# Third-operand norms and a reordered prologue in an adaLN state-space and FFN layer

## The chip, the cores and the metric

The kernel runs on one core of one Trainium2 chip. The metric is the device time of one execution in microseconds. The kernel before was timed in three runs: 542.87 us in the median, 541.35 to 543.33.

## The reference, cut to what matters

The layer has four batches of 512 tokens and 256 channels, all in fp32.

```python
mod = (_silu(L0_c) @ L0_wmod).reshape(L0_c.shape[0], 6, 1, -1)
sa, ca, ga, sb, cb, gb = (mod[:, 0], ..., mod[:, 5])
h = _layernorm(x, axis=-1) * (1 + ca) + sa
x = x + ga * _L0_attn_ref(h, W_in, conv_w, conv_b, z_bias, D, W_out)
h = _layernorm(x, axis=-1) * (1 + cb) + sb
x = x + gb * _L0_ffn_ref(h, W1, W2, W3)
```

The first sub-layer projects h to x (256 columns), to B and C (32 heads of 64 states each), to z and to one number per head, A. x, B and C go through a causal convolution of four taps along the tokens. a = -softplus(A), its running sums give decays exp(segsum(a)), and y is the sum over earlier tokens of (C . B) times the decay times x. Then y times silu(z) goes through W_out. The second sub-layer is a gated FFN with a Walsh-Hadamard transform in the hidden dimension of 1024. ga and gb are kept at least 0.25 away from zero.

## The kernel before, in words

Each engine has an order of work written out by hand, in its own block, and the engines meet through semaphores that count finished instructions. The program has three stages. The prologue (to about 56 us) normalises the input, computes h for all four batches, the x projection, its convolution, the projection A with its running sums and decays. The main loop goes over 16 half-groups of heads (NG groups, B batches each) in which B and C are projected, convolved and used. The last stage is the output projection, the second norm and the FFN.

In fp32 the products on TensorE are made of three passes. Every operand is split into a high part (rounded to the fast fp32r type) and a low part (the rest), and `split_mm` (L369) adds high weights x high h, high weights x low h, and low weights x high h. The parts of h are `ht_hi` and `ht_lo`; those of the x weights `wx_hi` and `wx_lo`.

The prologue, batch by batch, is a pipeline over the engines:

- VectorE: `statistics1(b)` (bn_stats, bn_aggr, variance + eps, L1053 to L1059), then `normalise1(b)` (L1066), four instructions of 128 x 256, that subtract the mean and multiply by `rstd`. `modulation(0)` copies shift and scale out of PSUM (L1096, L1097). Afterwards the taps of the x convolution (L1089), the softplus sum (`sp_a`, L1133), the scan of the running sums (L1137), and so on to the taps of the first B and C (L1177).
- GpSimd: `inverse_root(b)` (L1404) makes `rstd`, the weights of x are split at L1415 and L1417, `h_low(b, kt)` (L1409) makes the low part of h, `split_tile` (L1397, L1399) splits the weights of B and C, L1434 and L1436 those of z.
- TensorE: `norm_transposes(b)` (L396, eight transposes), filler products of zeros in `warm(n)` (L468), `x_project(b, xt)` (L410, six matmuls), `a_project(b0)` (L426, eight matmuls for two batches), `x_transposes`, `p_transposes` (L451, transposes of the running sums).
- ScalarE: `h_full(b, kt)` (L764) makes h in fp32 with scale and shift out of PSUM, `h_high(b, kt)` (L770) its high part, `x_tap(b, xt)` (L777) the last tap with bias. Then the absolute value (L810), exponential (L812) and logarithm (L815) of the softplus.

The waits that matter here: `h_full` waits for the transposes of its batch and for shift and scale (`mod_ev`); for batches 2 and 3 its slot of h32 has to be free too. `h_low` waits for `h_high`. `x_project(b, xt)` waits for both low parts of its batch, and from batch 2 on for the taps that read its PSUM bank two batches earlier. `a_project(2)` waits for h32 of batches 2 and 3. ScalarE's L810 waits for all the a products, and `x_tap(2, 0)` stands behind it in ScalarE's order.

The order on TensorE from the first transposes on is: transposes 0 and 1, ten fillers, `a_project(0)`, transposes 2, x of batch 0, transposes 3, x of batch 1, `a_project(2)`, `x_project(2, 0)`, the modulation for the second norm, and then transposes of x mixed with the rest of the x products and the transposes of the running sums. The second norm uses the same `normalise` helper, as `normalise2(b)`, once per batch (L1066 too), and its transposes are at L677.

Of the kernel before, what the change touches and what calls it, by code (L numbers as in the profile page):

```python
# [15 lines left out]
ALU = mybir.AluOpType  # L16
ACT = mybir.ActivationFunctionType

P = 128
B, L, D = 4, 512, 256  # L20
# [3 lines left out]
KT = D // P  # L24
# [4 lines left out]
GT = 4  # L29
# [21 lines left out]
def adaln_ssm_ffn_kernel(nc, u, w_bc, w_x, w_a, w_z, conv, d_rows, z_bias, w_out, w13, w2, c_t, wmod,  # L51
                         consts, out, e_d, gates_d):
    with ExitStack() as ctx:
        def sb(name, shape, dt, where=ctx):
            return where.enter_context(nc.sbuf_tensor(name, shape, dt))

        def sem(name):
            return ctx.enter_context(nc.semaphore(name))

        ps = ctx.enter_context(nc.psum_tensor("ps", [P, 8, BANK], F32))  # L60


        ht_hi = sb("ht_hi", [P, KT, B * L], F32R)
        ht_lo = sb("ht_lo", [P, KT, B * L], F32R)
# [12 lines left out]
        meanvar = sb("meanvar", [P, 2, CH, 2], F32)  # L77
        vareps = sb("vareps", [P, 2, CH], F32)
        rstd = sb("rstd", [P, 2, CH], F32)
# [14 lines left out]
        wx_hi = sb("wx_hi", [P, 2, KT, P], F32R, reg_a)  # L94
        wx_lo = sb("wx_lo", [P, 2, KT, P], F32R, reg_a)
# [45 lines left out]
        xt = sb("xt", [P, KT, L], F32)  # L141
# [32 lines left out]
        s = {n: sem(n) for n in names}  # L174
# [191 lines left out]
        def _(pe):  # L366
            mm = nc.tensor.matmul
# [21 lines left out]
            def norm_transposes(b):  # L389

                pe.wait_ge(s["xn_done"], CH * (b + 1))
                if b >= 2:
                    pe.wait_ge(s["h32_done"], KT * (2 * b - 3))
                for c in range(CH):
                    for kt in range(KT):
                        i = nc.tensor.transpose(ps[:, (4 if b == 1 else 2) + kt, c * P:(c + 1) * P],  # L396
                                                xn[:, b % 2, c, kt * P:(kt + 1) * P], ident)
                i.then_inc(s["lnT_mm"], 1)
# [11 lines left out]
            def x_project(b, xt):  # L410

                pe.wait_ge(s["hlo_done"], KT * (b + 1))
                if b >= 2:
                    pe.wait_ge(s[f"xtaps{xt}"], 3 * (b - 1))
                for kt in range(KT):
                    i = split_mm(ps[:, GT * (b % 2) + xt, :], wx_hi[:, xt, kt, :], wx_lo[:, xt, kt, :],
                                 ht_hi[:, kt, b * L:(b + 1) * L], ht_lo[:, kt, b * L:(b + 1) * L],
                                 kt == 0, kt == KT - 1)
                i.then_inc(s["xp_mm"], 1)

            def a_project(b0):

                pe.wait_ge(s["h32_done"], KT * (b0 + 2))
                for kt in range(KT):
                    for b in (b0, b0 + 1):
                        i = mm(ps[b * NH:(b + 1) * NH, 6, :], wa_sb[:, kt, :], h32[:, b % 2, kt, :],  # L426
                               start=(kt == 0), stop=(kt == KT - 1), skip_group_check=True)
                        if kt == KT - 1:
                            i.then_inc(s["a_mm"], 1)
# [35 lines left out]
            def warm(n):  # L465

                for k in range(n):
                    mm(ps[:, 1, :], zeros[:, 0:P], zeros[:], start=True, stop=True)  # L468
# [19 lines left out]
            pe.wait_ge(s["ld_ident"], 16)  # L488
            norm_transposes(0)
            norm_transposes(1)  # L490
            warm(10)
            pe.wait_ge(s["ld_wa"], 16)
            a_project(0)
            norm_transposes(2)
            pe.wait_ge(s["mod_ev"], 2)
            pe.wait_ge(s["wx_split"], 2)
            x_project(0, 0)
            x_project(0, 1)
            norm_transposes(3)
            x_project(1, 0)  # L500
            x_project(1, 1)
            a_project(2)
            x_project(2, 0)
            pe.wait_ge(s["ld_wmod2"], 16)
            modulation((3, 4), 7)
            x_transposes(0, 0)
# [244 lines left out]
        def _(act):  # L751
# [5 lines left out]
            def h_full(b, kt):  # L757

                n = KT * b + kt
                act.wait_ge(s["lnT_mm"], b + 1)  # L760
                if b >= 2:
                    act.wait_ge(s["hlo_done"], n - 3)
                    act.wait_ge(s["a_mm"], 2)
                af(h32[:, b % 2, kt, :], ps[:, (4 if b == 1 else 2) + kt, :], ACT.Identity, bias=shift[:, 0, kt, b:b + 1],  # L764
                   scale=scale1[:, 0, kt, b:b + 1]).then_inc(s["h32_done"], 1)

            def h_high(b, kt):

                act.wait_ge(s["h32_done"], KT * b + kt + 1)
                nc.scalar.copy(ht_hi[:, kt, b * L:(b + 1) * L], h32[:, b % 2, kt, :]).then_inc(s["hhi_done"], 1)  # L770

            def x_tap(b, xt):

                n = 2 * b + xt
                act.wait_ge(s["xp_mm"], n + 1)
                w = conv_sb[:, NG * GT + xt, :]
                af(acc[:, n // GT, n % GT, :], ps[:, GT * (b % 2) + xt, :], ACT.Identity, bias=w[:, TAPS:TAPS + 1],  # L777
                   scale=w[:, TAPS - 1:TAPS]).then_inc(s["xtap"], 1)
# [7 lines left out]

            act.wait_ge(s["mod_ev"], 2)
            h_full(0, 0)
            h_full(0, 1)
            h_full(1, 0)  # L790
            h_high(0, 0)
            h_full(1, 1)
            h_high(0, 1)
            h_high(1, 0)
            h_high(1, 1)
            h_full(2, 0)
            h_high(2, 0)
            h_full(2, 1)
            act.wait_ge(s["ld_conv"], 16)
            x_tap(0, 0)  # L800
            h_high(2, 1)
            x_tap(0, 1)
            h_full(3, 0)
            h_full(3, 1)
            x_tap(1, 0)
            x_tap(1, 1)
            h_high(3, 0)
            h_high(3, 1)
            act.wait_ge(s["a_mm"], B)
# [225 lines left out]
        def _(dve):  # L1035
            ts = nc.vector.tensor_scalar
            tt = nc.vector.tensor_tensor
            stt = nc.vector.scalar_tensor_tensor
# [22 lines left out]
            def normalise(src, dst, n, names):  # L1061

                st, ag, ep, rs, done = names
                dve.wait_ge(s[rs], n + 1)
                for c in range(CH):
                    ts(dst[:, c, :], src[:, c, :], meanvar[:, n % 2, c, 0:1], rstd[:, n % 2, c:c + 1], ALU.subtract,  # L1066
                       ALU.mult).then_inc(s[done], 1)

            norm1_names = ("bnst", "bnag", "eps1", "rs", "xn_done")
            norm2_names = ("bn2", "ag2", "eps2", "rs2", "xn2_done")  # L1070
# [5 lines left out]
            def normalise1(b):  # L1076
                if b >= 2:
                    dve.wait_ge(s["lnT_mm"], b - 1)
                normalise(u_sb[:, b * CH:(b + 1) * CH, :], xn[:, b % 2], b, norm1_names)
# [12 lines left out]
            def modulation(n):  # L1092

                dve.wait_ge(s["mod_mm"], 4 * (n + 1))
                mod = ps[:, 7 * n, 0:2 * KT * B].rearrange("p (k m b) -> p k m b", k=2, m=KT)
                nc.vector.tensor_copy(shift[:, n], mod[:, 0]).then_inc(s["mod_ev"], 1)  # L1096
                ts(scale1[:, n], mod[:, 1], 1.0, None, ALU.add).then_inc(s["mod_ev"], 1)  # L1097
# [10 lines left out]
            statistics1(0)  # L1108
            statistics1(1)
            normalise1(0)  # L1110
            normalise1(1)
            modulation(0)
            statistics1(2)
            statistics1(3)
            normalise1(2)
# [247 lines left out]
        def _(pool):  # L1363
# [28 lines left out]
            def split_tile(g, t):  # L1392

                if not (isinstance(g, int) and g == 0) and t < 2:
                    await_unit("w_high_act", g * 2 + PLACE[t] - 1)
                else:
                    gp.tensor_copy(wg_hi[:, t], wg_raw[:, t]).then_inc(s["w_high"], 1)  # L1397
                    await_unit("w_high", g * 2 + PLACE[t] + 1)
                gp.tensor_tensor(wg_lo[:, t], wg_raw[:, t], wg_hi[:, t].bitcast(F32), ALU.subtract).then_inc(s["w_split"], 1)  # L1399

            def inverse_root(n, eps_name, name):

                await_unit(eps_name, n + 1)
                gp.tensor_tensor(rstd[:, n % 2], vareps[:, n % 2], minus_half[:], ALU.pow).then_inc(s[name], 1)  # L1404

            def h_low(b, kt):

                pool.wait_ge(s["hhi_done"], KT * b + kt + 1)
                gp.tensor_tensor(ht_lo[:, kt, b * L:(b + 1) * L], h32[:, b % 2, kt, :],  # L1409
                                 ht_hi[:, kt, b * L:(b + 1) * L].bitcast(F32), ALU.subtract).then_inc(s["hlo_done"], 1)  # L1410
# [4 lines left out]
            gp.tensor_copy(wx_hi[:], wx_raw[:]).then_inc(s["wx_split"], 1)  # L1415
            pool.wait_ge(s["wx_split"], 1)
            gp.tensor_tensor(wx_lo[:], wx_raw[:], wx_hi[:].bitcast(F32), ALU.subtract).then_inc(s["wx_split"], 1)  # L1417
            inverse_root(2, "eps1", "rs")
            inverse_root(3, "eps1", "rs")
            h_low(0, 0)  # L1420
            h_low(0, 1)
            h_low(1, 0)
            h_low(1, 1)
            h_low(2, 0)
            pool.wait_ge(s["ld_wg"], 16)
            split_tile(0, 1)
            h_low(2, 1)
            split_tile(0, 0)
            h_low(3, 0)
# [229 lines left out]
```

## Time and profile before

| what | value |
|---|---|
| median of three runs | 542.87 us (541.35 to 543.33) |
| profiled execution | 541.1 us, span 538.9 us |
| mean granted clock of TensorE | 0.996 |
| TensorE busy | 528.2 us (98%) |
| VectorE busy | 455.3 us (84%) |
| ScalarE busy | 372.5 us (69%) |
| GpSimd busy | 241.0 us (45%) |
| one tap of a convolution on VectorE (L1177), mean of 384 | 0.741 us |

Busy time is the sum in which an engine had an instruction under way. A busy TensorE isn't one at its peak, since its matmuls overlap. The span is the time from the first to the last instruction of the profiled execution, and the rest of its time lies around it.

### The profile page before, as it was taken

To read this page: it belongs to the slowest core of one execution; us is meant where nothing else is said; L and a number is where in the kernel's file an instruction comes from. 1 tells how busy PE (TensorE), PEld (TensorE's weight loads), DVE (VectorE), ACT (ScalarE), POOL (GpSimd) and SP (SyncE) were. 2 spreads that over 40 slices of the span, in tenths; PEclk is the share of its full clock that TensorE was granted. 3 is DMA by queue.
4 is the path that set the end of the run, shared out by engine and by line. 5 is a ranking of instruction groups with operands and counts; after the bars stand their busy time and mean duration, and the time that the engine had idled before them with its cause. 6 is when DMAs were issued, how large, how long until landed. Compare 5 with 4: busy or idle time off the path is not lost.

```text
span 538.9 us, 19393 instructions
## 1 busy us (share of the span) xinstructions
PE 528.2 (98%) x7188; PEld 427.2 (79%) x7188; DVE 455.3 (84%) x746; ACT 372.5 (69%) x988; POOL 241.0 (45%) x465
## 2 busy tenths in 40 slices
PE   6999999999999999999999999999999999999997
PEld 3667777878878878877877877876889889889886
DVE  6999999999999999999999999999756657657342
ACT  1778998898898898898898898887534234234240
POOL 5863374776776775776775574484000000000000
PEclk9999999999999999999999999999999999999999
DMA  7737443432423425423423424566531322100101
GB/s 261 286 110 224 122 112 98 141 83 95 138 79 95 138 80 176 134 83 95 134 84 95 132 85 138 166 196 191 160 80 38 79 78 79 40 1 1 40 0 40
DMA packets 50289, 59.40 MB, mean 110 GB/s; under 512 B 8004, under 2 KB 44740, under 8 KB 49864
## 3 DMA queue, kind: packets, MB, share of 16 engines
q1 hardware_dynamic: 50248, 58.88, 36.0%
q8 instruction: 22, 0.36, 0.3%
q14 instruction: 19, 0.16, 0.1%
HBM read 48.75 MB, written 9.05 MB: 107 GB/s over the span
## 4 chain that ended last, share of the span: by engine, by line
PE 92%; DVE 4%; ACT 2%; issue 1%; DMA 1%; POOL 0%; SPq 0%; ACTq 0%; DVEq 0%; POOLq 0%
PE ps L371 20%; PE ps L372 20%; PE ps L373 20%; PE ps L550 10%; PE ps L531 6%; PE ps L600 4%; PE ps L586 3%; PE ps L569 3%; PE ps L667 3%; DVE acc L1177 2%; PE ps L396 1%; PE ps L613 1%; DMA u_sb<-in_u 1%; PE ps L426 1%; PE ps L677 1%
## 5 line engine op out<-in xcount | busy, mean ns | idle before, releaser
L1177 DVE SCALAR_TENSOR_TENSOR acc<-ps,cw_dve,acc 128x511 f32<-128x511 f32 (+2 forms) x384 | 257.8, 741 | 3.5 <-ACT acc L834 3.0
L868 ACT ACTIVATE decay<-sums,p_slot 128x128 f32<-128x128 f32 (+1 forms) x512 | 147.0, 370 | 2.2 <-ACT p_slot L943 1.0
L1478 POOL TENSOR_TENSOR sums<-sums,far_above 128x256 f32<-128x256 f32 x128 | 96.0, 753 | 117.4 <-DMA sums<-packed_sums 111.0
L834 ACT ACTIVATE acc<-ps,cw_act 128x512 f32<-128x512 f32 x128 | 93.0, 776 | 28.5 <-PE ps L600 26.4
L371 PE MATMUL ps<-ht_hi,wg_hi 128*128 128x512 f32 x256 | 107.1, 419 | 0.1
L372 PE MATMUL ps<-ht_lo,wg_hi 128*128 128x512 f32 x256 | 101.2, 395 | 0.0
L373 PE MATMUL ps<-ht_hi,wg_lo 128*128 128x512 f32 x256 | 101.2, 395 | 0.0
L1003 ACT ACTIVATE silu_sb<-ps 128x512 f32<-128x512 f32 x32 | 19.2, 599 | 77.8 <-PE ps L373 77.8
L1165 DVE TENSOR_TENSOR mix<-ps,decay 128x768 f32<-128x768 f32 x64 | 60.9, 952 | 6.1 <-PE ps L550 5.2
L1404 POOL TENSOR_TENSOR rstd<-vareps,minus_half 128x4 f32<-128x4 f32 x8 | 8.4, 1048 | 119.4 <-DVE vareps L1059 117.1
L550 PE MATMUL ps<-acc 64*64 64x128 f32 (+1 forms) x2048 | 57.6, 249 | 0.8
L373 PEld LDWEIGHTS ps<-ht_hi,wg_lo 128*128 128x128 f32 x256 | 48.1, 188 | 11.6
L1316 DVE TENSOR_TENSOR hid<-ps,silu_sb 128x512 f32<-128x512 f32 x32 | 22.1, 692 | 40.4 <-ACT silu_sb L1003 40.3
L371 PEld LDWEIGHTS ps<-ht_hi,wg_hi 128*128 128x128 f32 x256 | 48.2, 188 | 9.6 <-issue 0.4
L372 PEld LDWEIGHTS ps<-ht_lo,wg_hi 128*128 128x128 f32 x256 | 48.5, 189 | 8.5
L550 PEld LDWEIGHTS ps<-acc 64*64 64x64 f32 x2048 | 48.8, 133 | 7.0 <-issue 2.5
L371 PE MATMUL ps<-h_hi,w_hi 128*128 128x512 f32 x128 | 50.5, 394 | 0.0
L373 PE MATMUL ps<-h_hi,w_lo 128*128 128x512 f32 x128 | 49.9, 390 | 0.0
L372 PE MATMUL ps<-h_lo,w_hi 128*128 128x512 f32 x128 | 49.9, 390 | 0.0
L371 PE MATMUL ps<-w_hi,hid_hi 128*128 128x256 f32 x128 | 36.9, 289 | 0.2 <-DVE stage L1332 0.2
L372 PE MATMUL ps<-w_lo,hid_hi 128*128 128x256 f32 x128 | 36.2, 283 | 0.0
L373 PE MATMUL ps<-w_hi,hid_lo 128*128 128x256 f32 x128 | 36.2, 283 | 0.0
(143 smaller groups left out, 889.8 us busy)
## 6 DMA issues: line engine op xcount, KB each, us to landing
sums<-packed_sums SPq DMA_DIRECT2D x256, 96.0 KB, 2.7
wg_raw<-in_w_bc SPq DMA_DIRECT2D x8, 512.0 KB, 4.2
y_parts<-yt_sb SPq DMA_DIRECT2D x64, 64.0 KB, 2.0
stage<-y_parts SPq DMA_DIRECT2D x32, 128.0 KB, 2.8
u_sb<-in_u SPq DMA_DIRECT2D x4, 512.0 KB, 4.4
stage<-in_w SPq DMA_DIRECT2D x1, 2048.0 KB, 11.6
x_channels<-acc SPq DMA_DIRECT2D x8, 256.0 KB, 2.6
ee<-running_sums SPq DMA_DIRECT2D x8, 256.0 KB, 3.7
```

What stands on the lines that cost most here:

```text
L371: mm(o, w_hi, x_hi, start=first, stop=False)
L372: mm(o, w_hi, x_lo, start=False, stop=False)
L373: return mm(o, w_lo, x_hi, start=False, stop=last)
L531: i = nc.tensor.transpose(ps[:, 6, c * P:(c + 1) * P], acc[:, b % 2, p, c * P:(c + 1) * P], ident)
L550: i = mm(ps[NS * at:NS * (at + 1), 2 + a, o:o + P - NS * h], acc[own, b % 2, p, c * P + NS * h:c * P + NS * (h + 1)], acc[own, b % 2, 2 + ...
L600: i = mm(ps[QD * quarter:QD * (quarter + 1), 7, k * P + NS * h:(k + 1) * P], xs[:, b % 2, w:w + QD], mix[:, j, k * PW + NS * (1 - h):k * P ...
L834: af(acc[:, b % 2, t, :], ps[:, PROJ_BANK[t], :], ACT.Identity, bias=cw_act[:, t, 1:2], scale=cw_act[:, t, 0:1]).then_inc(s[f"tap_a{t}"], 1)
L868: i = af(decay[:, j, own], sums[:, j, own], ACT.Exp, scale=-1.0, bias=p_slot[:, b * CH + n, j:j + 1])
L1165: tt(mix[:, 2 * p:2 * p + 2, 0:PL], ps[:, 2:4, 0:PL], decay[:, 2 * p:2 * p + 2, 0:PL], ALU.mult).then_inc(s["mixed"], 1)
L1177: stt(a[:, d:], ps[:, PROJ_BANK[t], 0:L - d], cw_dve[:, t, TAPS - 1 - d:TAPS - d], a[:, d:], ALU.mult, ALU.add).then_inc(s[f"taps{t}"], 1)
L1316: tt(hid[:, m % 2, :], ps[:, 2 + m % 2, :], silu_sb[:, m % 2, :], ALU.mult).then_inc(s["hid_done"], 1)
L1478: gp.tensor_tensor(v, v, far, ALU.add).then_inc(s["masked"], 1)
```

## The change

It has five parts. (1) `normalise` uses scalar_tensor_tensor, with `rstd` broadcast along 256 columns as a third operand, instead of tensor_scalar with two per-partition scalars; the mean stays such a scalar. It serves both norms. (2) VectorE copies the modulation between the norms of batch 0 and batch 1. (3) On TensorE two new functions make the x product in two passes, first all that uses the high part of h, and later what uses the low part; batches 0 and 1 go by them. Six of ten fillers go, `a_project(0)` stands between the two passes of batch 0, transposes 2 behind them, and `x_project(2, 0)` ahead of `a_project(2)`. (4) ScalarE's order follows: the high part right behind the full one for batch 0, and the taps ahead of the next batch's h. (5) On GpSimd the low parts of batch 0 go in front of the inverse roots of batches 2 and 3, and the first weight split ahead of the low part (2, 0).

```diff
+            def x_project_high(b):
+                pe.wait_ge(s["hhi_done"], KT * (b + 1))
+                for xt in range(2):
+                    for kt in range(KT):
+                        o, x = ps[:, GT * (b % 2) + xt, :], ht_hi[:, kt, b * L:(b + 1) * L]
+                        mm(o, wx_hi[:, xt, kt, :], x, start=(kt == 0), stop=False, skip_group_check=True)
+                        mm(o, wx_lo[:, xt, kt, :], x, start=False, stop=False, skip_group_check=True)
+            def x_project_low(b):
+                pe.wait_ge(s["hlo_done"], KT * (b + 1))
+                for xt in range(2):
+                    for kt in range(KT):
+                        i = mm(ps[:, GT * (b % 2) + xt, :], wx_hi[:, xt, kt, :], ht_lo[:, kt, b * L:(b + 1) * L],
+                               start=False, stop=(kt == KT - 1), skip_group_check=True)
+                    i.then_inc(s["xp_mm"], 1)
...
             norm_transposes(1)
-            warm(10)
+            warm(4)
+            pe.wait_ge(s["mod_ev"], 2)
+            pe.wait_ge(s["wx_split"], 2)
+            x_project_high(0)
             pe.wait_ge(s["ld_wa"], 16)
             a_project(0)
+            x_project_low(0)
             norm_transposes(2)
-            pe.wait_ge(s["mod_ev"], 2)
-            pe.wait_ge(s["wx_split"], 2)
-            x_project(0, 0)
-            x_project(0, 1)
+            x_project_high(1)
+            x_project_low(1)
             norm_transposes(3)
-            x_project(1, 0)
-            x_project(1, 1)
+            x_project(2, 0)
             a_project(2)
-            x_project(2, 0)
...
             h_full(0, 0)
+            h_high(0, 0)
             h_full(0, 1)
+            h_high(0, 1)
             h_full(1, 0)
-            h_high(0, 0)
             h_full(1, 1)
-            h_high(0, 1)
             h_high(1, 0)
             h_high(1, 1)
-            h_full(2, 0)
-            h_high(2, 0)
-            h_full(2, 1)
             act.wait_ge(s["ld_conv"], 16)
             x_tap(0, 0)
+            x_tap(0, 1)
+            h_full(2, 0)
+            h_full(2, 1)
+            h_high(2, 0)
             h_high(2, 1)
-            x_tap(0, 1)
+            x_tap(1, 0)
+            x_tap(1, 1)
             h_full(3, 0)
             h_full(3, 1)
-            x_tap(1, 0)
-            x_tap(1, 1)
...
-                    ts(dst[:, c, :], src[:, c, :], meanvar[:, n % 2, c, 0:1], rstd[:, n % 2, c:c + 1], ALU.subtract,
-                       ALU.mult).then_inc(s[done], 1)
+                    stt(dst[:, c, :], src[:, c, :], meanvar[:, n % 2, c, 0:1], rstd[:, n % 2, c:c + 1].to_broadcast([P, D]),
+                        ALU.subtract, ALU.mult).then_inc(s[done], 1)
...
             normalise1(0)
+            modulation(0)
             normalise1(1)
-            modulation(0)
...
+            h_low(0, 0)
             inverse_root(2, "eps1", "rs")
+            h_low(0, 1)
             inverse_root(3, "eps1", "rs")
-            h_low(0, 0)
-            h_low(0, 1)
             h_low(1, 0)
             h_low(1, 1)
-            h_low(2, 0)
             pool.wait_ge(s["ld_wg"], 16)
             split_tile(0, 1)
+            h_low(2, 0)
             h_low(2, 1)
```

## Rows read from the trace of the kernel before

**Rows 1.** The page, the chain that ended last, by engine.

```profile
PE 92%; DVE 4%; ACT 2%; issue 1%; DMA 1%; POOL 0%; SPq 0%; ACTq 0%; DVEq 0%; POOLq 0%
```

**Rows 2.** Stages: length; PE, PEld, DVE, ACT, POOL busy (instructions); clock, DMA share, GB/s.

```profile
12.84:14.60 1.76, 1.76 (x8) 1.70 (x9) 1.73 (x10) 1.45 (x2) 0.00 (x0) 0.50 1.02 389
14.60:17.60 3.00, 3.00 (x13) 1.10 (x11) 2.96 (x13) 2.75 (x5) 1.68 (x2) 0.76 0.66 250
...
67.00:357.00 290.00, 289.37 (x5329) 232.72 (x5333) 281.21 (x405) 258.14 (x766) 190.27 (x384) 1.00 0.38 114
```

**Rows 3.** Timeline of TensorE: start, length, line, count, idle before.

```profile
12.84 1.97 PE L396 MATMUL ps<-cst,xn 128*128 128x128 f32 x8 [1.45 <-DVE xn L1066]
14.60 3.04 PE L468 MATMUL ps<-sums 128*128 128x512 bf16 x10
17.58 1.91 PE L426 MATMUL ps<-h,wa_sb 128*32 128x512 f32 x8
19.42 1.09 PE L396 MATMUL ps<-cst,xn 128*128 128x128 f32 x8
20.62 0.47 PE L371 MATMUL ps<-ht_hi,wx_hi 128*128 128x512 f32 x1
...
23.51 1.03 PE L396 MATMUL ps<-cst,xn 128*128 128x128 f32 x8
...
27.29 1.91 PE L426 MATMUL ps<-h,wa_sb 128*32 128x512 f32 x8
...
35.73 1.09 PE L451 MATMUL ps<-cst,sums_t 128*64 128x128 f32 x16 [0.19 <-DVE sums_t L1137]
```

**Rows 4.** Timeline of VectorE, the norms, the taps and the scan.

```profile
8.80 3.99 DVE L1066 TENSOR_SCALAR xn<-u_sb,meanvar,rstd 128x256 f32<-128x256 f32 x8
...
10.72 1.42 DVE L1066 TENSOR_SCALAR xn<-u_sb,meanvar,rstd 128x256 f32<-128x256 f32 x1
...
18.20 5.01 DVE L1066 TENSOR_SCALAR xn<-u_sb,meanvar,rstd 128x256 f32<-128x256 f32 x4 [0.15 <-POOL rstd L1404]
...
34.37 1.22 DVE L1137 TENSOR_TENSOR_SCAN sums_t<-reset,sp_a 128x512 f32<-128x512 f32 x1
...
43.76 7.31 DVE L1177 SCALAR_TENSOR_TENSOR acc<-ps,cw_dve,acc 128x511 f32<-128x511 f32 x11 [0.23 <-ACT acc L834]
```

**Rows 5.** Line L1066 alone (ns min/median/max), and ScalarE's timeline.

```profile
L1066 DVE TENSOR_SCALAR xn<-x_tok,meanvar,rstd x16: 406/408/411, 375.4 to 492.6; 128x256 f32<-128x256 f32 x16
...
15.52 0.61 ACT L770 CAST ht_hi<-h 128x512 fp32r<-128x512 f32 x1
16.03 0.78 ACT L764 ACTIVATE h<-ps,shift,scale 128x512 f32<-128x512 f32 x1
...
29.27 0.60 ACT L810 ACTIVATE a_work<-ps 128x512 f32<-128x512 f32 x1
...
30.84 0.78 ACT L777 ACTIVATE acc<-ps,conv_sb 128x512 f32<-128x512 f32 x1 [0.30 <-PE ps L373]
```

**Rows 6.** A third-operand form on VectorE, GpSimd beside it, and line L1478.

```profile
354.64 0.74 DVE L1198 SCALAR_TENSOR_TENSOR stage<-xt,d_ch,stage 128x512 f32<-128x512 f32 x1
...
360.10 1.00 DVE L1198 SCALAR_TENSOR_TENSOR stage<-xt,d_ch,stage 128x512 f32<-128x512 f32 x1
...
360.50 1.20 POOL L1478 TENSOR_TENSOR sums<-sums,far_above 128x256 f32<-128x256 f32 x1
...
L1478 POOL TENSOR_TENSOR sums<-sums,far_above x128: 724/738/1286, 42.3 to 371.3; 128x256 f32<-128x256 f32 x128
```

**Rows 7.** Timeline of GpSimd: weight splits and low parts.

```profile
10.73 1.26 POOL L1417 TENSOR_TENSOR wx_lo<-wx_raw,wx_hi 128x512 fp32r<-128x512 f32 x1
...
17.92 6.44 POOL L1409 TENSOR_TENSOR ht_lo<-h,ht_hi 128x512 fp32r<-128x512 f32 x5
...
34.45 2.20 POOL L1436 TENSOR_TENSOR wz_lo<-wz_raw,wz_hi 128x512 fp32r<-128x512 f32 x1
```

**Rows 8.** Waits from 360 us on: total, times, longest.

```profile
PEld ps L677 <- DVE xn L1066: 0.2, 1, 0.2
```

## The prediction

> **What bounds the kernel now.** I read the chain of waits first: 92% of it is TensorE's [rows 1]. The stage table then shows TensorE busy for 289.37 of 290.00 us in the main loop, with VectorE at 281.21 [rows 2]. All the edits but the second norm's lie ahead of that loop, so they can only move the moment at which it begins, and the time is as long as that moment is late. The timeline of TensorE comes next. From 12.84 us on it has next to no idle time, but not all of it is needed: ten filler products run from 14.60 to 17.6 us (3.04 us, 0.30 each), because the first x product waits for the low part of h [rows 3]. The granted clock is low there: 0.50 from 12.84 to 14.60 us and 0.76 over 14.60 to 17.60, that is 1.2 GHz first and 2.4 GHz later. TensorE sat idle for 1.45 us ahead of it, from 11.39 to 12.84 us [rows 2, 3]. VectorE is the other one without slack: it is delayed in the fourth norm (four instructions in 5.01 us, where the 16 of the later norm take 0.41 us each) and then runs taps almost without a break, until the scan at 34.37 us releases TensorE's transposes at 35.73 us and eleven taps from 43.76 us on lie in the chain [rows 3, 4, 5]. So TensorE's order, VectorE's order and the softplus chain (a products, ScalarE, scan, transposes) are nearly co-critical, and an edit has to move all three forward to gain.
>
> **The norm with a third operand.** The nearest row of that form is the 128x512 one at 354.64 us: 0.74 us [rows 6]. Half of its columns, at 0.96 a ns, are 0.27 us, so 128x256 takes about 0.48. Eleven taps of 0.741 us (table of the profile) fill 7.31 us, so instructions start 0.66 apart and overlap by 0.08 [rows 4]: 0.40 from start to start, against 0.41 less 0.08, 0.33, now. That is +0.07 us each. Bounds: 0 (it costs what tensor_scalar costs) and 0.33 (the 512-column form whole).
>
> What could pay for it is VectorE no longer standing behind GpSimd. The rows show that standing: one norm instruction takes 1.42 us beside the split of wx (1.26 us), and the fourth norm's four take 5.01 us beside low parts of 1.29 us [rows 4, 7]. But instructions that read two SBUF tensors stand in the same way: the 128x512 form took 1.00 us at 360.10 beside GpSimd work, and the GpSimd mask at 360.50 took 1.20 against a median of 0.738 us; the scan at 34.37 ran beside a GpSimd subtraction of 2.20 us whose twin takes 1.26 [rows 4, 6, 7]. The new form reads two SBUF tensors (u_sb and the broadcast rstd). I take it that it is held too, and, being longer, holds GpSimd by about 0.1 us more.
>
> The Trainium skill ("SBUF — State Buffer", section "SBUF: two separate sides") says that the port pair of VectorE and GpSimd is an exclusive lock, taken by a VectorE instruction in a two-port mode or with two SBUF inputs against a GpSimd instruction that reads SBUF. By that rule the third operand takes the norm out of one clause and puts it into the other; the rows above agree.
>
> In time: the first norm ends at 8.80 + 3 x 0.40 + 0.48 = 10.48 us, against 10.18 (8.80 + 3 x 0.32 + 0.41). The modulation copies (two, of 8 columns each) go next, so they are done at 10.6 instead of 12.9 us. Of the second norm's four, the first starts at 10.6 and pushes the split of wx from about 11.99 to 12.3 us, the second ends at 12.6, the others at 13.0 and 13.4. The second transposes start at 13.5 instead of 12.84 us: +0.65.
>
> **The x products with high h first, and the low parts in front.** ScalarE may start at 11.7 us, when the first transposes are done (11.39 + 0.3). A full h is 0.78 us, a high part 0.61, and now each high part waits for its full one: both high parts of batch 0 stand at about 11.7 + 2 x (0.78 + 0.61) = 14.5 us [rows 5]. TensorE isn't there yet: transposes 1.76 us at the low clock to 15.26, four fillers at 0.43 (twice the 0.213 that 512 columns take at 2.4 GHz) to 17.0. Then eight high products at 0.24 (twelve take 2.89 [rows 3]) to 18.9, the a products 1.84 to 20.7, four low products 0.95 to 21.7. The low part of h is ready long before: GpSimd had nothing to do from 12.84 to 14.60 us [rows 2], where the low part (0, 0) goes (1.29 us), and (0, 1) follows the third inverse root and ends near 17.6 us. So its wait is gone. No DMA is moved and SyncE's order is the same. The fourth inverse root comes later by what is left of that low part, about 0.7 us. The fourth norm, which ended at 18.20 + 5.01 = 23.2 us, I expect to end near 23.6; the fourth transposes need it at 25.6, and x_project(2, 0) needs the fifth tap behind it, at 23.6 + 5 x 0.66 = 26.9. Both are covered, by 2 and by 0.5 us; past that each us costs a us.
>
> What is late next are the third transposes. They stood behind the a products alone and ended at 20.5 us; now they stand behind both x parts as well and end at 21.7 + 1.03 = 22.7 us [rows 3]. So h of batch 2 is 2.2 us later: full parts 22.75 to 24.2 (overlapping by 0.1), high parts to 25.3, low parts 24.8 to 27.4 (2 x 1.29). The first weight split has moved ahead of them and ends before 24.8. TensorE in that time does x of batch 1 (12 x 0.24) and the fourth transposes, to about 26.5, then idles 0.9 us, where it had no wait at all. x_project(2, 0) runs 27.4 to 28.85 us.
>
> **The a products moved behind it.** They used to run from 27.29 to 27.29 + 1.84 = 29.13 us; now from 28.85 to 30.7 [rows 3], +1.55. ScalarE's absolute value and exponential wait for them and x_tap(2, 0) behind those: it began 1.57 us after the absolute value, 0.30 of that idle, so 30.75 + 1.27 = 32.0 instead of 30.84 us, then the table load and the logarithm [rows 5]. So the idle 0.30 takes in a part of the +1.55, and 0.1 is rounding. The three taps, sp_a and the scan follow, so the transposes of the sums start at 35.73 + 1.15 = 36.9 us. From there the order on every engine is as before, and neither has idle time to take it in. Bounds: 0 (x of batch 2 not late) and 1.6 (nothing taken in).
>
> **The norms of the second half.** +0.07 x 4 per batch. TensorE waits once for this norm, 0.2 us, at batch 0, and not at the others, which are hidden by the down projection [rows 8]. So up to 0.3 there; I take 0.2.
>
> **Sum.** +1.15 + 0.2 = +1.35. The profiled execution took 541.1 us (span 538.9), 1.8 below the median of 542.87; 541.1 + 1.35 = 542.45, on the median's footing 544.2. A measurement can tell about 0.5% here, 2.7 us, so I call this no change, on the slow side.
>
> **Rivals.**
> *A wash.* The third operand is not held by GpSimd. The second norm ends at 10.6 + 3 x 0.40 + 0.48 = 12.3, its transposes start at 12.4, x of batch 0 is done by 12.4 + 1.76 + 1.7 + 1.9 + 1.84 + 0.95 = 20.5, 1.2 us ahead of the forecast, so the a products of batch 2 end at 29.5 instead of 29.13 us; VectorE leaves the fourth norm near 19.5. With 0.2 for the later norm the end is +0.2 to +0.4: 543.1 us. For it: nothing but the different form; against it the three cases in the rows. 0.20.
>
> *The fillers come off whole.* Six fillers at 0.30 are 1.8 us of TensorE's gapless stretch. If the second transposes are not later and the batch-2 chain finds cover, all behind moves by -1.8, with the later norm -1.6: 541.3 us. For it speaks that TensorE has no idle time between 12.84 and 35.5; against it that VectorE and the a products must come forward too. 0.15.
>
> *The slow side: the clock stays low.* The idle time ahead of the second transposes grows from 1.45 to 1.8 us and there are six fewer fillers, so that the products of x run at 1.2 GHz: the eight high ones cost 1.9 us more, which is paid in full since TensorE paces the third transposes. It decides from the point where the granted clock is still at 0.5 after 17.0 us. 544.2 + 1.9 = 546.1 us. For it: the clock was low behind such a gap [rows 2]; against it: it came back within the fillers' stretch, and the work is as dense. 0.12.
>
> **How the numbers follow.** Forecast 0.50, wash 0.20, fillers 0.15, low clock 0.12, others 0.03. The range is 541.0 to 546.1: the fillers' case to the low clock's, with half a us of run noise below. Slower by over 0.5% (above 545.6): half of the low-clock case, a tenth of the forecast: 0.11. Faster by over 0.5% (below 540.2): a third of the fillers' case and a little noise, 0.06. Within: 0.83.
>
> **What would show it.** Norm instructions near 0.48 us alone and 1.3 to 1.5 us beside GpSimd's low parts; the second transposes at 13.5; third transposes ending at 22.7; a gap on TensorE ahead of x_project(2, 0), released by a low part; the scan at 35.5. The forecast is wrong if norms beside low parts take 0.5 us, if the scan starts at or before 34.4, or if the time falls below 542.

## The result and the profile after

The changed kernel took 543.12 us in the median of 22 runs (542.0 to 544.14), the kernel before 541.71 us in 22 (540.62 to 543.65). The ratio is 1.0023, 95% interval [1.0014, 1.0032]: 1.2 us slower, 0.8 to 1.7. The forecast was +1.35. The three runs of the prediction had put the kernel before at 542.87 us, 1.2 above its median of 22, so only differences are compared below, and not times. The profiled execution took 542.87 us, its span is 540.7.

TensorE's timeline after the change (start, length, line, count, idle before and its releaser); x_project_high is at L427 and L428, x_project_low at L435, the a products at L444, the transposes of the sums at L469:

```profile
10.75 1.06 PE L396 MATMUL ps<-cst,xn 128*128 128x128 f32 x8 [1.84 <-DVE xn L1084]
13.61 1.97 PE L396 MATMUL ps<-cst,xn 128*128 128x128 f32 x8 [1.79 <-DVE xn L1084]
15.37 1.60 PE L486 MATMUL ps<-sums 128*128 128x512 bf16 x4
16.62 0.58 PE L427 MATMUL ps<-ht_hi,wx_hi 128*128 128x512 f32 x1
...
18.76 1.91 PE L444 MATMUL ps<-h,wa_sb 128*32 128x512 f32 x8
20.60 1.18 PE L435 MATMUL ps<-ht_lo,wx_hi 128*128 128x512 f32 x4
21.62 1.03 PE L396 MATMUL ps<-cst,xn 128*128 128x128 f32 x8
...
27.44 0.48 PE L371 MATMUL ps<-ht_hi,wx_hi 128*128 128x512 f32 x1 [1.10 <-POOL ht_lo L1427]
...
37.04 1.09 PE L469 MATMUL ps<-cst,sums_t 128*64 128x128 f32 x16 [1.73 <-DVE sums_t L1155]
```

Against [rows 3]: the idle time ahead of the second transposes is 1.79 instead of 1.45 us, there is a new gap of 1.10 us ahead of x_project(2, 0), released by a low part, and one of 1.73 us ahead of the transposes of the sums, where 0.19 stood. Those start 1.31 us later than before.

VectorE, and its norm line (ns min/median/max):

```profile
8.94 1.67 DVE L1084 SCALAR_TENSOR_TENSOR xn<-u_sb,meanvar,rstd 128x256 f32<-128x256 f32 x4
...
10.67 2.88 DVE L1084 SCALAR_TENSOR_TENSOR xn<-u_sb,meanvar,rstd 128x256 f32<-128x256 f32 x4
...
17.78 5.97 DVE L1084 SCALAR_TENSOR_TENSOR xn<-u_sb,meanvar,rstd 128x256 f32<-128x256 f32 x8
...
32.96 2.06 DVE L1107 SCALAR_TENSOR_TENSOR acc<-ps,conv_sb,acc 128x511 f32<-128x511 f32 x3 [1.73 <-ACT acc L795]
...
L1084 DVE SCALAR_TENSOR_TENSOR xn<-u_sb,meanvar,rstd x16: 473/479/1511, 8.9 to 22.8; 128x256 f32<-128x256 f32 x16
```

GpSimd's low parts (two in 2.92 us beside the norm) and its line of all eight:

```profile
19.10 2.92 POOL L1427 TENSOR_TENSOR ht_lo<-h,ht_hi 128x512 fp32r<-128x512 f32 x2
...
L1427 POOL TENSOR_TENSOR ht_lo<-h,ht_hi x8: 1272/1290/1479, 13.4 to 32.3; 128x512 fp32r<-128x512 f32 x8
```

The new form takes 0.479 us alone and up to 1.51 beside GpSimd, where tensor_scalar had 0.41 and 1.42 [rows 4, 5], and the low part beside it takes 1.48 instead of 1.29. I call an instruction held when it is longer than alone because it has to wait for the other engine. The granted clock, by stretch:

```profile
13.30:15.10 1.80, 1.49 (x7) 1.50 (x8) 1.80 (x9) 1.34 (x3) 1.28 (x1) 0.50 1.05 415
15.10:17.00 1.90, 1.90 (x8) 1.05 (x7) 1.86 (x10) 1.39 (x3) 1.42 (x2) 0.62 0.72 196
```

An estimate from these rows and from [rows 2]: 0.50 over 1.80 us and 0.62 over 1.90 are 1.80 + 1.44 = 3.2 us at 1.2 GHz, and in the kernel before 1.76 + 1.44 = 3.2 as well (0.50 over 1.76 us, 0.76 over 3.00). In these two executions the low stretch has the same length, and only comes about 0.5 us later.

The main loop is as it was (289.45 of 290 us busy). Not all of the 1.8 us between the spans is the prologue's. The first norm starts 0.14 us later, at 8.94, before anything changed is met, and at the loop's end 0.67 us of waiting for a tap stand where there was none:

```profile
361.24 0.47 PE L371 MATMUL ps<-ht_hi,wz_hi 128*128 128x512 f32 x1 [0.67 <-DVE acc L1195]
```

That wait was 0.15 us or absent in the profiles of the experiments, so I take it to belong to that execution. I therefore compare prologues by the distance from the first norm instruction to the transposes of the sums.

### The profile page after: what moved, and what is told of

Read it like the earlier page. It is cut to its first block, busy times and chain, and to the rows that moved or that the text cites. A ratio compares the mean times of both kernels' runs of the same rounds, so it can differ in the third digit from the quotient of the medians.

```text
span 540.7 us, 19381 instructions
## 1 busy us (share of the span) xinstructions
PE 526.2 (97%) x7182; PEld 426.8 (79%) x7182; DVE 457.0 (85%) x746; ACT 372.2 (69%) x988; POOL 240.5 (44%) x465
## 4 chain that ended last, share of the span: by engine, by line
PE 90%; DVE 5%; ACT 2%; issue 1%; DMA 1%; POOL 0%; SPq 0%; DVEq 0%; ACTq 0%
PE ps L371 20%; PE ps L372 19%; PE ps L373 19%; PE ps L568 9%; PE ps L549 5%; PE ps L618 4%; PE ps L587 3%; PE ps L604 3%; PE ps L685 3%; DVE acc L1195 2%; DVE xn L1084 1%; DMA u_sb<-in_u 1%; PE ps L631 1%; PE ps L695 1%; PE ps L444 1%
## 5 line engine op out<-in xcount | busy, mean ns | idle before, releaser
L1496 POOL TENSOR_TENSOR sums<-sums,far_above 128x256 f32<-128x256 f32 x128 | 94.4, 741 | 120.5 <-DMA sums<-packed_sums 112.1
L371 PE MATMUL ps<-w_hi,hid_hi 128*128 128x256 f32 x128 | 36.9, 289 | 0.2 <-DVE stage L1350 0.2
```

Of the source, the lines that this page charges most:

```text
L371: mm(o, w_hi, x_hi, start=first, stop=False)
L1496: gp.tensor_tensor(v, v, far, ALU.add).then_inc(s["masked"], 1)
```

## The experiments

"Distance" is that distance in the one profiled execution, against 26.93 us in the kernel before (35.73 - 8.80), and "clock" the mean granted clock of that execution (0.996 in the kernel before): a distance also holds what the clock cost there. "Total" is the ratio's distance from 1 times 541.7 us.

| kernel | ratio to the kernel before, 95% | total, us | distance, against before | clock |
|---|---|---|---|---|
| changed | 1.0023 [1.0014, 1.0032] | +1.2 | 28.10, +1.2 | 0.997 |
| e1 third operand alone | 1.0027 [1.0016, 1.0039] | +1.5 | 28.12, +1.2 | 0.994 |
| e2 changed, scalar norms | 0.9990 [0.9976, 1.0004] | -0.5 | 26.19, -0.7 | 1.000 |
| e3 changed, a products first | 1.0027 [1.0007, 1.0046] | +1.5 | 28.0, +1.1 | 0.996 |
| e4 changed, operand in PSUM | 0.9987 [0.9978, 0.9997] | -0.7 | 26.70, -0.2 | 0.997 |
| e5 e2, no overlap in norm 1 | 0.9976 [0.9965, 0.9986] | -1.3 | 25.87, -1.1 | 1.000 |
| e6 e5, reordered for batch 2 | 1.0003 [0.9990, 1.0016] | +0.2 | 28.45, +1.5 | 0.996 |
| e7 changed, ten fillers | 1.0036 [1.0023, 1.0049] | +2.0 | 29.64, +2.7 | 0.997 |
| e8 changed, tap before softplus | 1.0015 [1.0005, 1.0025] | +0.8 | 28.69, +1.8 | 0.993 |
| e9 e5, taps and h of batch 2 interleaved | 0.9986 [0.9976, 0.9996] | -0.8 | 25.90, -1.0 | 1.000 |
| e10 changed, no overlap in norm 1 | 1.0020 [1.0007, 1.0032] | +1.1 | 28.24, +1.3 | 1.000 |
| e11 e9, scan without overlap | 0.9976 [0.9965, 0.9987] | -1.3 | 25.91, -1.0 | 0.995 |
| e12 before, no overlap in norm 1 | 0.9982 [0.9968, 0.9996] | -1.0 | 26.13, -0.8 | 1.000 |

**e1, the third operand alone.**

```diff
 (kernel before)
-                    ts(dst[:, c, :], src[:, c, :], meanvar[..., 0:1], rstd[..., c:c + 1], ALU.subtract, ALU.mult)
+                    stt(dst[:, c, :], src[:, c, :], meanvar[..., 0:1], rstd[..., c:c + 1].to_broadcast([P, D]),
+                        ALU.subtract, ALU.mult)
```

> The kernel before with the one edit of the third operand in both norms. Theory (the new form is held by GpSimd as the old one was, and is longer): the second transposes start about 0.6 us later than 12.84, the fourth norm takes 5.9 us instead of 5.01 and each low part beside it 1.46 instead of 1.29 us, and the total is +0.8 to +1.2 us against the kernel before. Rival (all the loss is the order of the a products): 0.0 to +0.2 us. Second rival (the new form is free of GpSimd): the fourth norm takes 1.7 us, and the total is -0.3 to +0.2.

Measured: +1.5 us. The second transposes start at 13.35, the third and fourth norm together take

```profile
17.12 7.36 DVE L1066 SCALAR_TENSOR_TENSOR xn<-u_sb,meanvar,rstd 128x256 f32<-128x256 f32 x8
```

where they took 1.38 and 5.01 us. The two had started at 16.67 us and ended at 23.21 there, gap included. So this one edit makes as much as the whole change, and a little more than I had expected of it (0.8 to 1.2).

**e2, scalar norms in the changed order.** The edit of e1 undone in the changed kernel.

> The changed kernel with tensor_scalar back in both norms, all else changed. Theory: the second transposes start 0.6 us earlier than in the changed kernel (13.0), and the whole chain down to the scan moves with them: -0.5 to -0.8 us against the changed kernel, still +0.4 to +0.7 above the kernel before. Rival (order of the a products alone): no difference from the changed kernel.

Measured: -0.5 us against the kernel before (interval from -1.3 to +0.2), so about 1.8 us below the changed kernel, more than twice what I had expected. The transposes are 0.6 us earlier, as said; what I had not counted is in these rows:

```profile
13.07 1.09 PE L396 MATMUL ps<-cst,xn 128*128 128x128 f32 x8 [1.46 <-DVE xn L1084]
...
18.77 3.17 DVE L1084 TENSOR_SCALAR xn<-u_sb,meanvar,rstd 128x256 f32<-128x256 f32 x4 [0.16 <-POOL rstd L1422]
...
25.62 0.47 PE L371 MATMUL ps<-ht_hi,wx_hi 128*128 128x512 f32 x1 [1.21 <-DVE acc L1107]
```

The fourth norm ends near 21.9 instead of 23.7 us and frees VectorE for the taps, which are now what x_project(2, 0) waits for; and the transposes ran at 2.4 GHz in this execution (1.09 instead of 1.97 us). The mean granted clock was 1.000 in 6 of 11 runs (540.3 to 541.1 us) and 0.994 or 0.996 in the others (541.7 to 542.6). Of the changed kernel's 22 runs none had 1.000, and ten had 0.993 (543.0 to 543.7 us).

**e3, the a products first.**

```diff
 (changed kernel)
-            x_project(2, 0)
             a_project(2)
+            x_project(2, 0)
```

> The changed kernel with a_project(2) back in front of x_project(2, 0). a_project(2) then waits for the full h of batch 3, at 27.9 us, and ends at 29.8 instead of 31.0; x_project(2, 0) ends at 31.3, x_tap(2, 0) starts near 31.4 instead of 32.2, and the scan moves by the same. Theory (the softplus chain sets the end): -0.6 to -0.9 us against the changed kernel. Rival (TensorE's sum of work sets it): 0 to +0.4, since TensorE now idles 1.5 us instead of 1.1 ahead of these products.

Measured: +1.5 us against the kernel before, no gain on the changed one; the interval is wide (seven runs). The a products run earlier, but into a wait for h of batch 3, and VectorE's scan is longer:

```profile
27.94 1.91 PE L444 MATMUL ps<-h,wa_sb 128*32 128x512 f32 x8 [1.63 <-ACT h L782]
...
36.67 1.09 PE L469 MATMUL ps<-cst,sums_t 128*64 128x128 f32 x16 [0.73 <-DVE sums_t L1155]
```

```profile
35.01 1.51 DVE L1155 TENSOR_TENSOR_SCAN sums_t<-reset,sp_a 128x512 f32<-128x512 f32 x1
```

The scan starts 0.4 us nearer to the first norm than in the changed kernel (26.35 against 26.74), but it takes 1.51 us instead of 1.21, since it stood behind GpSimd's subtraction for the z weights. The expectation of -0.6 to -0.9 fell.

**e4, the third operand in PSUM.** The first norm multiplies by zeros left in PSUM by the first fillers; the multiplication by rstd is left out in it.

```diff
 (changed kernel)
-            warm(20)
+            warm(20, 7).then_inc(s["filled"], 1)
...
+                    factor = ps[:, 7, 0:D] if done == "xn_done" else rstd[:, n % 2, c:c + 1].to_broadcast([P, D])
```

> The changed kernel, but the third operand of the first norm is read from PSUM (zeros of the first twenty fillers, now in bank 7) in place of rstd, so the multiplication by rstd is left out there; the instruction has the same form and length and one SBUF input. Theory (two SBUF inputs are what holds it): 0.48 us each also beside GpSimd work, the second norm ends near 12.3, the fourth takes 1.7 us, low parts take 1.29 us, the second transposes start at 12.4 instead of 13.6: -1.0 to -1.3 us against the changed kernel. Rival (any long VectorE instruction that reads SBUF is held): as the changed kernel.

Measured: -0.7 us against the kernel before, about 1.9 below the changed one, more than the 1.0 to 1.3 expected. The same form, with one SBUF tensor instead of two:

```profile
L1088 DVE SCALAR_TENSOR_TENSOR xn<-u_sb,meanvar,ps x16: 470/472/479, 9.0 to 20.3; 128x256 f32<-128x256 f32 x16
...
17.54 3.22 DVE L1088 SCALAR_TENSOR_TENSOR xn<-u_sb,meanvar,ps 128x256 f32<-128x256 f32 x8
```

```profile
18.79 2.53 POOL L1431 TENSOR_TENSOR ht_lo<-h,ht_hi 128x512 fp32r<-128x512 f32 x2
```

No instruction of sixteen is held (479 ns at most, 1511 in the changed kernel), and the low parts beside them are back at 1.27 us. That is the mechanism shown: it is the second SBUF input that meets GpSimd, not the length or the form. The edit also takes the broadcast away, but that isn't what is held: the scan (L1155) reads two whole SBUF tensors, and takes 1.51 us in e3 and 1.66 in e8 beside a GpSimd subtraction, where it takes 1.21 alone. Since everything behind this norm works on other numbers in e4, I lean on the length of its instructions and less on its total. The Trainium skill ("SBUF — State Buffer", section "SBUF: two separate sides") states the lock for just this case, two SBUF inputs against a GpSimd instruction that reads SBUF. This trace agrees, with 1511 ns at most for two SBUF inputs and 479 for one. What the change took out by leaving tensor_scalar's form, which was held too (1.42 us), it put back with the broadcast operand.

**e5, no overlap in the second norm.**

```diff
 (e2)
+            act.wait_ge(s["ld_wx"], 16)
+            nc.scalar.copy(wx_hi[:], wx_raw[:]).then_inc(s["wx_split"], 1)
...
-            gp.tensor_copy(wx_hi[:], wx_raw[:]).then_inc(s["wx_split"], 1)
+            pool.wait_ge(s["xn_done"], 2 * CH)
```

> tensor_scalar norms in the changed order; ScalarE (idle there) makes the high part of the x weights, and GpSimd starts their low part only when the second norm is done. Theory (what VectorE loses to GpSimd in the second norm sets the start of the second transposes): they start at 12.1 to 12.3 us instead of 13.07 in the kernel with scalar norms, the gap on TensorE ahead of them shrinks from 1.45 to 0.6 us, and the granted clock stays nearer 1.0; behind that h of batch 0 (ready at 14.5) sets the high x products, so -0.3 to -0.8 us against that kernel, -0.8 to -1.3 against the kernel before. Rival (later steps set all): no difference from the kernel with scalar norms.

Measured: -1.3 us against the kernel before, as expected. The gap ahead of the second transposes is 0.30 us, and the clock was 1.000 in 8 of 12 runs:

```profile
11.69 1.09 PE L396 MATMUL ps<-cst,xn 128*128 128x128 f32 x8 [0.30 <-DVE xn L1086]
...
34.67 1.09 PE L469 MATMUL ps<-cst,sums_t 128*64 128x128 f32 x16 [1.72 <-DVE sums_t L1157]
```

**e6, reordered for batch 2.** e5 with the third transposes ahead of x_project_low(0), h of batch 2 ahead of the taps of batch 0 on ScalarE, the low parts of batch 2 ahead of the first weight split, x_tap(2, 0) ahead of the absolute value.

> As the last one, with the third transposes ahead of x_project_low(0), ScalarE's h of batch 2 ahead of the taps of batch 0, the low parts of batch 2 ahead of the first weight split, and x_tap(2, 0) ahead of the absolute value. Theory (the changed kernel loses on the way third transposes, h of batch 2, x_project(2, 0), a products, scan): no gap ahead of x_project(2, 0), transposes of the sums at 33.5 to 34.3 instead of 35.73 us in the kernel before, total -1.5 to -2.3 us against the kernel before. Rival (VectorE's taps set it): they start at 21 to 22 us and the transposes of the sums come at 35 or later, total -0.8 or less.

Measured: +0.2 us against the kernel before, so 1.5 us worse than e5. The low part was ready at 24.5 us, and x_project(2, 0) waited for its PSUM bank instead:

```profile
26.92 0.47 PE L371 MATMUL ps<-ht_hi,wx_hi 128*128 128x512 f32 x1 [2.51 <-DVE acc L1109]
```

```profile
23.14 9.54 DVE L1109 SCALAR_TENSOR_TENSOR acc<-ps,conv_sb,acc 128x511 f32<-128x511 f32 x14 [1.25 <-ACT acc L795]
```

The taps of batch 0 had been put behind h on ScalarE; the rival named that. Behind that wait the granted clock fell once more, from about 27.7 to 31 us (0.50 over 28.00 to 31.00), and four of the a products took 1.59 us there, where they take 1.03 in the changed kernel:

```profile
29.96 1.59 PE L444 MATMUL ps<-h,wa_sb 128*32 128x512 f32 x4
```

How much of the 1.5 us is the wait and how much the clock, no run tells.

**e7, ten fillers.** `warm(10)` for `warm(4)` in the changed kernel.

> The changed kernel with ten fillers instead of four. Theory (TensorE paces the way to the third transposes): the high x products start 1.3 to 2.0 us later and the whole is +1.3 to +1.8 us against the changed kernel. Rival (the fillers keep the clock up and pay for themselves): the mean granted clock is higher than in the changed kernel (0.993 in half of its runs) and the total within 0.5 us of it.

Measured, by five runs: +2.0 us against the kernel before, 0.7 above the changed one, with clocks of 0.997 in four of them. The distance grows by 1.5 us in the one profile. The loss lies between the two expectations. The fillers delay the x products, and the higher mean clock did not pay for them: the four runs at 0.997 took 544.0 to 544.5 us and the fifth, at 0.993, 543.3.

**e8, x_tap(2, 0) ahead of the softplus.**

```diff
 (changed kernel)
+            x_tap(2, 0)
             act.wait_ge(s["a_mm"], B)
...
-            x_tap(2, 0)
             act.wait_ge(s["aexp_done"], 1)
```

> The changed kernel with one move: ScalarE's x_tap(2, 0) ahead of the absolute value, which waits for the a products. Theory (VectorE's idle 1.7 us ahead of its three taps and sp_a behind them are on the path): the idle time goes, sp_a starts when the logarithm ends, 34.2 instead of 34.94 us, and the total is -0.5 to -0.8 us against the changed kernel; a collision of the scan with the split of the z weights, as it cost 0.3 us with the a products first, may take back 0.3. Rival (the a products alone set it): 0.

Measured: +0.8 us against the kernel before, 0.4 below the changed kernel, with intervals that overlap. The expected 0.5 to 0.8 isn't shown. The distance is long because the profiled execution had the clock at 1.2 GHz until about 18.4 us (mean 0.993), which delayed the x products; it says nothing of the edit. VectorE's idle time moved behind the taps, and the collision I had named was larger, 0.45 instead of 0.3 us:

```profile
35.07 0.69 DVE L1151 SCALAR_TENSOR_TENSOR sp_a<-ps,a_work 128x512 f32<-128x512 f32 x1 [1.91 <-ACT a_work L833]
...
35.82 1.66 DVE L1155 TENSOR_TENSOR_SCAN sums_t<-reset,sp_a 128x512 f32<-128x512 f32 x1
```

**e9, taps and h interleaved.** e5 with the third transposes ahead of x_project_low(0), ScalarE's full h (2, 0), (2, 1), high (2, 0), tap (0, 0), high (2, 1), tap (0, 1), VectorE's taps of (0, 0) first, and the low parts of batch 2 ahead of the first weight split.

> The kernel with scalar norms and no overlap in the second norm, with the third transposes ahead of x_project_low(0), ScalarE's order full h (2, 0), (2, 1), high (2, 0), tap (0, 0), high (2, 1), tap (0, 1), VectorE's three taps of (0, 0) first, and the low parts of batch 2 ahead of the first weight split. Theory (x_project(2, 0) is held by two waits, the low part and the PSUM bank that the taps of (0, 0) still read, and both must move): it starts at 24.1 to 24.4 instead of 25.07 us and the transposes of the sums come 0.5 to 0.9 us earlier than in that kernel; total -1.6 to -2.1 us against the kernel before. Rival (VectorE, which now idles until 22.1 us, or the waits behind 50 us take it back): -1.3 or less.

Measured: -0.8 us against the kernel before; the interval overlaps that of e5. x_project(2, 0) starts at 24.41, but then the scan takes 1.67 us beside GpSimd. The gain stays below 1.3 us as the rival said, and the scan's hold is what the trace shows for it.

**e10, third operand without overlap in the second norm.** The edit of e5 in the changed kernel.

> The changed kernel, third operand kept, but ScalarE makes the high part of the x weights and GpSimd starts their low part behind the second norm. Theory (the third operand costs by its hold in the second norm and so by the start of the second transposes; its hold in the fourth norm is covered): the second norm takes 1.67 us, the second transposes start at 12.6 instead of 13.6 us, -0.8 to -1.2 us against the changed kernel, near the kernel before. Rival (the fourth norm's hold, 6 us, is what costs): no gain against the changed kernel.

Measured: +1.1 us, no gain that shows on the changed kernel; my expectation fell, and the rival, the fourth norm's hold, held. The second transposes do start at 12.00, but

```profile
27.19 0.47 PE L371 MATMUL ps<-ht_hi,wx_hi 128*128 128x512 f32 x1 [2.40 <-DVE acc L1109]
```

```profile
17.51 5.99 DVE L1086 SCALAR_TENSOR_TENSOR xn<-u_sb,meanvar,rstd 128x256 f32<-128x256 f32 x8
```

the hold in the third and fourth norm is as long as before, the taps start at 23.4 us, and x_project(2, 0) waits for them. This execution ran at 2.4 GHz throughout the prologue, and still the transposes of the sums come 1.3 us later than in the kernel before. In the changed kernel x_project(2, 0) waited for a low part, behind the late second transposes, and here it waits for the taps, behind the fourth norm. So the third operand costs on two parallel ways, and with the one over the second norm shortened the other keeps the time as it is. The converse, the second norm held and the fourth free, was not run.

**e11, the scan without overlap.** e9, with GpSimd's low part of the z weights behind `sums_done`.

> The last scalar-norm kernel (h of batch 2 and taps interleaved) with one wait more: GpSimd's low part of the z weights starts only when the scan is done. Theory (the scan reads two SBUF tensors and is held by that GpSimd subtraction, 1.67 instead of 1.22 us): the scan takes 1.22 us, the transposes of the sums come 0.45 us earlier, -0.3 to -0.5 us against that kernel, -1.3 to -1.8 against the kernel before. Rival (something behind the scan sets the loop's begin): no difference from that kernel.

Measured: the scan takes 1.21 us; -1.3 us against the kernel before. The gain on e9 lies inside the intervals. The distance shows none because e9 was profiled at a clock of 1.000 and e11 with its second transposes at 1.2 GHz (1.97 instead of 1.09 us).

**e12, no overlap in the second norm, old order.** The edit of e5 in the kernel before.

> The kernel before (its order, ten fillers, tensor_scalar norms) with only the x weights' high part on ScalarE and their low part behind the second norm. Theory (in the old order x of batch 0 waits for a low part that stands behind the fourth inverse root, so an earlier second norm helps only by earlier statistics of batch 3): x of batch 0 starts 0.4 to 0.8 us earlier, total -0.3 to -0.8 us. Rival (the order is what gains in the kernel with both, -1.3 us): 0.

Measured: -1.0 us against the kernel before, a little above the expected range, and not told apart from e5. The rival, that only the new order lets this edit gain, fell. Here x of batch 0 waits 1.42 us for a low part:

```profile
19.98 0.47 PE L371 MATMUL ps<-ht_hi,wx_hi 128*128 128x512 f32 x1 [1.42 <-POOL ht_lo L1411]
```

## Why the prediction was right, and which of its terms were not

The size, the sign and the way were right: +1.35 forecast, +1.2 [0.8, 1.7] measured. Point by point:

- *The new form's price.* 0.48 us alone was forecast, 0.479 found. That it is held by GpSimd was forecast and e4 shows why.
- *The second transposes.* Forecast 13.5; 13.61 at an origin 0.14 later. Right.
- *Third transposes, h of batch 2, x_project(2, 0).* Forecast ends of 22.7 and a start at 27.4 behind a low part; found 22.65 (21.62 + 1.03) and 27.44, released by a low part. Right.
- *The transposes of the sums.* Forecast 36.9, found 37.04, the 0.14 being the origin. The prologue's +1.15 was found as +1.17 (28.10 against 26.93).
- *The later norm, +0.2.* Too large: its transposes start 0.96 us after the products ahead of them in both profiles, and TensorE's wait for this norm grew from 0.2 [rows 8] to 0.3 us. At most 0.1 us is owed to it.
- *How the sum divides.* This was the step at fault. I took the order as the loss and the operand as a part of it: a(2) behind x_project(2, 0) for most of the +1.15, and only the 0.65 of the second transposes for the operand. The runs give the third operand alone +1.5 (e1) or 1.8 (changed against e2), and the order -0.5, which by itself isn't told from nothing. I had noted that the fourth norm is covered by 0.5 us of slack; e10 shows how thin that cover was: with the first hold gone, the second takes its place at once. That the forecast met the total although it divided it wrongly is in part luck. e3 doesn't show what the place of a_project(2) is worth: the scan came 0.4 us earlier, a collision took 0.3 of it back, and the total's interval is 2 us wide.
- *The rival of the low clock.* It was given 0.12, and little of it is true: the products of x did not run at 1.2 GHz (eight in 2.1 us), and the low stretch is as long as before. The mean clock does differ between the kernels. 12 of 22 runs of the changed kernel have 0.994 or less, against 35 of the 104 runs of the kernel before that lie beside the experiments, and none has 1.000, against 22 of the 104. But at like clocks the distance stays: the middle is 542.5 against 541.3 us at 0.995 to 0.997, and 543.4 against 542.4 at 0.994 or less. 55% of the runs instead of 34% in a group that is 1.0 us longer make 0.2 us: by this estimate so much of the +1.2 comes with the clock, and the rest without it.
- *The fillers' rival* had 0.15. In e2, where VectorE comes forward too, at most a part of the six fillers shows, -0.5 us with nothing inside the interval. e5's -1.3 isn't the fillers' either, as e12 keeps all ten and has -1.0.

e5, e9, e11 and e12 compute the same as the kernel before and are faster than it beyond their intervals, e5 and e11 by most, at -1.3 us [-1.9, -0.7] or 0.24%. e12 has -1.0 with three new lines and one fewer. These four aren't told apart from each other.

## What to carry to other kernels

A change of instruction form that is meant to keep VectorE out of GpSimd's way has to be judged by where its operands lie: with two tensors in SBUF it is held as before and takes longer itself (0.48 instead of 0.41 us here), with one of them in PSUM it wasn't held at all (e4). It is safer to move the GpSimd work out of that stretch, here onto an idle ScalarE. And where two waits of nearly the same length guard one product, an experiment that removes one shows nothing; both have to go before either can be priced.

## What the runs showed of the hardware that was not expected

The mean granted clock of one kernel differs from run to run; over all the kernels it lies between 0.989 and 1.000. In the profiles TensorE is at 1.2 GHz for one stretch between 10 and 18.5 us or for none, in e6 for one near 29 us behind its wait of 2.51 us, and in e11 also for the last 1.6 us, when TensorE had nothing left to do. In e2 the runs at 1.000 took 540.3 to 541.1 us, those at 0.994 or 0.996 took 541.7 to 542.6. With an edit worth 1 us this is as large as the edit, so the clocks of the runs have to be read beside their times. But the mean doesn't say which work lay in the low stretch, and e7 shows longer times at 0.997 than at 0.993.

What brings the low stretch is open. The kernels with the third operand in SBUF have 1.000 in one run of 68, the experiments without it in 30 of 82. In e5, with gaps of 1.05, 0.30 and 0.75 us on TensorE around its first transposes, 8 of 12 runs had it, and in the changed kernel, with 1.84 and 1.79, none of 22. But e10, with 1.14, 0.57 and 1.19, had it in one of 12, and the kernel before, with 1.51 and 1.45, in 22 of 104.

The hold goes both ways. tensor_scalar beside the low parts left them near 1.29 us (five in 6.44 [rows 7]), the longer form stretched one to 1.48, and a 512-column scan stretched a 512-column subtraction from 1.29 to 2.20 us [rows 7] when it came first, and was itself stretched from 1.22 to 1.66 (e8) when it came second.
